# Mixture-of-experts layer on one core: rows added to the output by accumulating DMAs, in place of a last stage of gathers

## What is computed

```python
def _L0_ffn_ref(x, gamma, beta, Wr, br, W1, b1, W2, b2):
    ...
    logits = jnp.einsum('bsd,de->bse', xn, Wr) + br
    top_vals, top_idx = jax.lax.top_k(logits, K)          # K = 2
    w = jax.nn.softmax(top_vals, axis=-1)
    w_full = jnp.einsum('bsk,bske->bse', w, jax.nn.one_hot(top_idx, E, dtype=w.dtype))
    y = jnp.zeros(x.shape[:-1] + (DOUT,), x.dtype)
    for e in range(E):                                     # E = 8
        h = jax.nn.gelu(jnp.einsum('bsd,dh->bsh', xn, W1[e]) + b1[e], approximate=False)
        y_e = jnp.einsum('bsh,hd->bsd', h, W2[e]) + b2[e]
        y = y + y_e * w_full[..., e, None]
    return y
...
x = x + _L0_ffn_ref(_layernorm(x, axis=-1)[None], ...)[0]
```

## Time and profile before

| | us |
|---|---|
| median of 3 runs | 5577.97 (5570.27 to 5583.16) |
| the profiled execution | 5578.17 |
| its span, first to last instruction | 5576.4 |
| scatter of the rows (L1738 to L1742), first to last start | 4108.2 to 4427.3 |
| expert loop, first transpose to last bias add | 4468.7 to 5236.0 |
| last stage (`finish`), first POOL copy to the end of the span | 5238.2 to 5576.4 |

### The profile page before, as it was taken

How to read it: one execution, slowest core, us unless ns; L and a number is a source line. 1 busy time by engine, 2 the same in 40 slices (tenths; PEclk the granted TensorE clock), 3 DMA queues, 4 the chain that set the end, 5 groups by cost and what they waited for, 6 DMA issues and landing times. The chain is left out here.

```text
span 5576.4 us, 84757 instructions
## 1 busy us (share of the span) xinstructions
PE 3167.4 (57%) x17248; PEld 2502.8 (45%) x17249; DVE 2738.4 (49%) x6553; ACT 1159.1 (21%) x3323; POOL 2454.4 (44%) x2678
## 2 busy tenths in 40 slices
PE   4998066666666666777755551014410099999500
PEld 3775044444444555555544441003300089999500
DVE  6555344444555555666667777862220034444322
ACT  2443011111111222222211112322200023333100
POOL 3000277777777777777722223430036400000266
PEclk9999577787888888889966665555555599999755
DMA  4111644444444444444423332221123422222243
GB/s 135 57 57 59 224 125 121 121 121 121 122 123 121 121 123 123 126 125 126 125 86 91 95 91 83 81 63 38 38 72 120 143 80 71 71 70 71 85 116 112
DMA packets 427990, 564.92 MB, mean 101 GB/s; under 512 B 78180, under 2 KB 362676, under 8 KB 427806
## 3 DMA queue, kind: packets, MB, share of 16 engines
q0 software_dynamic: 94528, 263.96, 16.9%
q1 hardware_dynamic: 292398, 261.14, 16.2%
q10 hardware_dynamic: 41040, 39.59, 2.1%
HBM read 420.77 MB, written 144.88 MB: 101 GB/s over the span
## 5 line engine op out<-in xcount | busy, mean ns | idle before, releaser
L993 POOL DMA_INDIRECT rows<-node_rows,index x1564 | 1668.8, 1067 | 529.7 <-issue 468.8
L1131 PE MATMUL ps_sum<-msg,hot 128*128 128x260 f32 x3904 | 1226.7, 468 | 17.8 <-DVE big L1074 0.3
L1131 PEld LDWEIGHTS ps_sum<-msg,hot 128*128 128x128 f32 x3904 | 859.0, 232 | 179.8 <-issue 27.9
L1110 PE MATMUL ps_hot<-ident_h,hotT 128*128 128x128 bf16 x1952 | 224.7, 247 | 763.4 <-DVE hotT L1041 700.8
L1041 DVE TENSOR_SCALAR hotT<-targets,pair_node_id 128x512 bf16 x488 | 185.5, 380 | 940.5 <-SPq L956 939.1
L1065 DVE TENSOR_TENSOR msg<-rows,msg 128x1024 f32<-128x1024 f32 x488 | 601.8, 1233 | 75.4 <-ACT msg L1093 57.8
L1110 PEld LDWEIGHTS ps_hot<-ident_h,hotT 128*128 128x128 bf16 x1952 | 148.3, 110 | 942.2 <-DVE hotT L1041 684.2
L1088 ACT ACTIVATE e<-e 128x16 f32<-128x16 f32 x488 | 105.2, 216 | 1575.5 <-DVE e L1059 1570.2
L1881 DVE COPY x_rowsT<-x_ps_t 128x256 f32<-128x256 f32 x204 | 86.6, 425 | 652.1 <-PE x_ps_t L1835 652.1
L1845 PEld LDWEIGHTS x_ps_hT<-x_rowsT,x_w_now 128*128 128x128 f32 x3264 | 398.4, 193 | 12.1 <-DVE x_w_now L1892 1.7
L1845 PE MATMUL x_ps_hT<-x_rowsT,x_w_now 128*128 128x128 f32 x3264 | 399.5, 276 | 1.3 <-DVE x_w_now L1892 1.3
(11 more groups left out here) (256 smaller groups left out, 5010.4 us busy)
## 6 DMA issues: line engine op xcount, KB each, us to landing
targets<-dst_row SPq DMA_DIRECT2D x391, 128.0 KB
expert_in<-c_zeros ACTq DMA_DIRECT2D x51, 512.0 KB, 8.1
x_rows<-expert_in SPq DMA_DIRECT2D x204, 128.0 KB, 2.1
expert_out<-x_outs SPq DMA_DIRECT2D x204, 128.0 KB, 1.7
rows<-node_rows,index POOLq DMA_INDIRECT x1564
node_rows<-h_out SPq DMA_DIRECT2D x98, 132.0 KB
h_row<-node_rows SPq DMA_DIRECT2D x98, 132.0 KB, 2.1
queries<-q_out SPq DMA_DIRECT2D x98, 128.0 KB
```

What stands on the lines that cost most here:

```text
L993: g.indirect_dma_start(rows[:, j, k, :], None, s.node_rows, bass.IndirectOffsetOnAxis(ap=index[:, b, j * G + k:j * G + k + 1], axis=0)).th ...
L1110: mm = pe.transpose(ps_hot[:, j % 2, k * P:(k + 1) * P], hotT[:, j % 2, k * P:(k + 1) * P], ident_h[:, :])
L1131: mm = pe.matmul(ps_sum[:, j % 2, 0:SUM], hot[:, j % MSGS, k * P:(k + 1) * P], msg[:, j % MSGS, k, :], start=(k == 0), stop=(k == G - 1))
```

## The change

The output is now formed by additions in DRAM.

- `join` stores each finished tile of `s.sums` to the output, 98 stores on SP's queue.
- Each row in `expert_in` is four numbers longer (1,040 bytes): the number of its node, its first choice of expert, and its two weights. `route` makes this tag for all nodes, and POOL copies it behind each row before the scatter. Blank rows carry a node number past the end (12,500 plus the row's place in the tile), and the output has 128 spare rows for them.
- In the expert loop VectorE picks the weight that belongs to the tile's expert (`gates`, `choose`, `weigh`), scales the bias with it (`weigh_bias`), and `add_bias` becomes product plus weight times sum in one operation. POOL adds the 128 finished rows to the output with one indirect DMA that accumulates (`add_rows`).
- Two tiles of one expert never hold the same node, tiles of different experts may. So before an add POOL waits until all adds of the experts before are done: `adds_before` is that number per tile, and SP counts the landed adds (`track`) into `adds_done`. For the tiles after the last expert's each waits for the one before.
- `expert_out`, its stores, and the whole stage `finish` are gone. The buffers `b2_b`, `bias` and `outs` now lie in `s.big`, which is free by then.

```diff
+BLANK_TILES = 4
+XW = D + 4
...
-    s.expert_in = nc.dram_tensor("expert_in", [EX_TILES * P, D], F32).ap()
-    s.expert_out = nc.dram_tensor("expert_out", [EX_TILES * P, D], F32).ap()
+    s.expert_in = nc.dram_tensor("expert_in", [EX_TILES * P, XW], F32).ap()
...
+                g.iota(blank[:, :, D:D + 1].bitcast(I32).rearrange("p t o -> p (t o)"), [[0, BLANK_TILES]], base=N,
+                       channel_multiplier=1).then_inc(blank_set, 1)
...
+                def store(t, rows):
+                    sp.dma_start(out[bass.ds(t * P, rows), :], s.sums[0:rows, bass.ds(t, 1), 0:D].rearrange("p t d -> p (t d)")).then_inc(stored, 16)
+
+                load(0, 0, P)
+                load(1, 1, P)
+                with sp.Fori(2, TILES - 3, 2) as t0:
+                    for u in range(2):
+                        load(t0 + u, u, P)
+                        store(t0 + (u - 2), P)
                 load(TILES - 2, 0, P)
+                store(TILES - 4, P)
                 load(TILES - 1, 1, TAIL)
+                store(TILES - 3, P)
+                for t in (TILES - 2, TILES - 1):
+                    sp.wait_ge(tile_done, t + 3)
+                    store(t, P if t < TILES - 1 else TAIL)
+                sp.wait_ge(stored, 16 * TILES)
...
+                done(v.tensor_copy(s.tag[:, :, 2], gap[:, :]))
+                done(v.tensor_tensor(s.tag[:, :, 3], odds[:, :], gap[:, :], ALU.mult))
+                done(v.tensor_scalar(s.tag[:, :, 1], lowest[:, 0, :], float(EXPERTS), None, ALU.add))
...
+                    done(v.scalar_tensor_tensor(owner[:, 1 - e % 2, :], tile_id[:, :], tile_end[:, e:e + 1], owner[:, e % 2, :], ALU.is_ge, ALU.add))
+                done(v.tensor_scalar(s.expert_f[:, :], owner[:, EXPERTS % 2, :], float(EXPERTS - 1), None, ALU.min))
+                done(v.tensor_copy(s.expert_of[0:1, :], s.expert_f[0:1, :]))
+
+                for e in range(EXPERTS):
+                    done(v.tensor_scalar(owner[0:1, 0, :], tile_id[0:1, :], tile_end[0:1, e:e + 1], tiles_f[0:1, e:e + 1], ALU.is_ge, ALU.mult))
+                    done(v.tensor_tensor(first_tile[:, 1 - e % 2, :], first_tile[:, e % 2, :], owner[0:1, 0, :], ALU.add))
+                done(v.tensor_scalar(owner[0:1, 0, :], tile_id[0:1, :], tile_end[0:1, EXPERTS - 1:EXPERTS], 0.0, ALU.subtract, ALU.max))
+                done(v.tensor_tensor(first_tile[:, EXPERTS % 2, :], first_tile[:, EXPERTS % 2, :], owner[0:1, 0, :], ALU.add))
+                done(v.tensor_scalar(s.adds_before[0:1, :], first_tile[:, EXPERTS % 2, :], float(EX_TILES), None, ALU.min))
...
-                    g.wait_ge(indexed, t + 1)
+                    g.tensor_copy(rows[:, j, D:XW], s.tag[:, bass.ds(t, 1), :].rearrange("p t k -> p (t k)")).then_inc(indexed, 1)
+                    g.wait_ge(indexed, t * 2 + 2)
...
+                sp.sem_inc(adds_done, 1)
 
                 def load(n, j, turn):
 
                     row = fixed(sp, n * P)
                     from_item(sp, rowsT_psum, n, EX_RING, n - EX_RING + 1)
+                    from_item(sp, tags_read, n, EX_RING, n * 2 - 2 * EX_RING + 2)
                     sp.dma_start(rows[:, j, :], s.expert_in[bass.ds(row, P), :]).then_inc(loaded[j], 16)
 
-                def store(n, j, turn):
-                    row = fixed(sp, n * P)
-                    sp.wait_ge(out_ready, n + 1)
-                    sp.dma_start(s.expert_out[bass.ds(row, P), :], outs[:, j, :]).then_inc(stored[j], 16)
-
-                in_tiles(sp, [load, store], [0, EX_HEAD])
+                def track(n, j, turn):
+                    sp.wait_ge(added[j], turn * 16 + 16)
+                    sp.sem_inc(adds_done, 1)
+
+                in_tiles(sp, [load, track], [0, TRACK])
+
+            WEIGHTS = 16 * (EXPERTS * (2 + HC) + 1)
+
+            @block.gpsimd
+            def _(g):
+                def add_rows(n, j, turn):
+                    before = g.value_load(s.adds_before[0:1, bass.ds(n, 1)], min_val=1, max_val=EX_TILES)
+                    g.wait_ge(out_ready, n + 1)
+                    g.wait_ge(adds_done, before)
+                    g.sem_inc(s.wait_seen, 1)
+                    g.indirect_dma_start(out, bass.IndirectOffsetOnAxis(ap=token[:, j:j + 1], axis=0),
+                                         outs[:, j, :], None, compute_op=ALU.add).then_inc(added[j], 16)
+
+                in_tiles(g, [add_rows], [0])
                 for j in range(EX_RING):
-                    sp.wait_ge(stored[j], 16 * (EX_TILES // EX_RING))
-
-            WEIGHTS = 16 * (EXPERTS * (2 + HC) + 1)
+                    g.wait_ge(added[j], 16 * (EX_TILES // EX_RING))
...
-                def add_bias(n, j, turn):
-                    e = expert(v, n)
-                    v.wait_ge(out_psum, n + 1)
-                    from_item(v, stored[j], n, EX_RING, turn * 16)
-                    v.tensor_tensor(outs[:, j, :], ps_out[:, j % 2, 0:D], flat(b2_b, e, slice(0, D)), ALU.add).then_inc(out_ready, 1)
...
-                in_tiles(v, [copy_rowsT, place_w1, add_bias], [0, 0, 3])
-
-
-def finish(nc, s, out):
...
+                def gates(n, j, turn):
+
+                    v.wait_ge(loaded[j], turn * 16 + 16)
+                    v.tensor_tensor(gap[:, j:j + 1], rows[:, j, D + 2:D + 3], rows[:, j, D + 3:D + 4], ALU.subtract).then_inc(halfway, 1)
+                    v.tensor_copy(second[:, j:j + 1], rows[:, j, D + 3:D + 4]).then_inc(tags_read, 1)
+
+                def choose(n, j, turn):
+                    v.wait_ge(halfway, n * 2 + 1)
+                    v.tensor_scalar(part[:, j:j + 1], rows[:, j, D + 1:D + 2], s.expert_f[:, bass.ds(n, 1)], gap[:, j:j + 1],
+                                    ALU.is_equal, ALU.mult).then_inc(halfway, 1)
+
+                def weigh(n, j, turn):
+                    v.wait_ge(halfway, n * 2 + 2)
+                    v.wait_ge(tags_read, n * 2 + 1)
+                    v.tensor_tensor(weight[:, j:j + 1], part[:, j:j + 1], second[:, j:j + 1], ALU.add).then_inc(weighted, 1)
+                    from_item(v, added[j], n, EX_RING, turn * 16)
+                    v.tensor_copy(token[:, j:j + 1], rows[:, j, D:D + 1].bitcast(I32)).then_inc(tags_read, 1)
+
+                def weigh_bias(n, j, turn):
+                    e = expert(v, n)
+                    v.wait_ge(weighted, n + 1)
+                    v.tensor_scalar(bias[:, j, :], flat(b2_b, e, slice(0, D)), weight[:, j:j + 1], None, ALU.mult).then_inc(bias_ready, 1)
+
+                def add_bias(n, j, turn):
+                    v.wait_ge(bias_ready, n + 1)
+                    v.wait_ge(out_psum, n + 1)
+                    from_item(v, added[j], n, EX_RING, turn * 16)
+                    v.scalar_tensor_tensor(outs[:, j, :], ps_out[:, j % 2, 0:D], weight[:, j:j + 1], bias[:, j, :],
+                                           ALU.mult, ALU.add).then_inc(out_ready, 1)
+
+                in_tiles(v, [gates, copy_rowsT, choose, place_w1, weigh, add_bias, weigh_bias], [0, 0, 0, 0, 0, 3, 2])
```

More of the change, by code:

```diff
@@ L881, in _, with attend_edges @@
                                            ALU.mult, ALU.max).then_inc(step, 1)
-def attend_edges(nc, s, plan):
+def attend_edges(nc, s, plan, out):
     with ExitStack() as ctx:
@@ L1093, in weights @@
                     act.activation(msg[:, j % MSGS, :, D:SUM], e4[:, j % 2, :, :], ACT.Exp, scale=-1.0).then_inc(w_ready, 1)
[L1095 to L1098 removed]
+                act.wait_ge(blank_set, 2)
+                for a in range(0, EX_TILES, BLANK_TILES):
+                    b = min(a + BLANK_TILES, EX_TILES)
+                    act.dma_start(s.expert_in[a * P:b * P, :].rearrange("(t p) d -> p t d", p=P), blank[:, 0:b - a, :]).then_inc(blank_stored, 16)
+                act.dma_start(out[N:N + P, :], blank[:, 0, 0:D]).then_inc(blank_stored, 16)
                 in_pairs(act, [bound, copy_hot, weights], [1, 0, 1])
[L1100 removed]
+                act.wait_ge(blank_stored, 16 * (-(-EX_TILES // BLANK_TILES) + 1))
             @block.tensor
@@ L1328, in _, with join @@
                         v.sem_inc(tile_done, 1)
-def join(nc, s, x, gamma, beta, w_norm2):
+def join(nc, s, x, gamma, beta, w_norm2, out):
     with ExitStack() as ctx:
@@ L1510, in route @@
         earlier = sb("earlier", [P, P])
-        tile_id = sb("tile_id", [1, EX_TILES])
-        owner = sb("f_owner", [1, 2, EX_TILES])
+        tile_id = sb("tile_id", [P, EX_TILES])
+        owner = sb("f_owner", [P, 2, EX_TILES])
+        first_tile = sb("f_first_tile", [1, 2, EX_TILES])
         ps_t = psum("f_ps_t")
@@ L1728, in load @@
                         from_item(sp, scattered[j][k], t, 4, times)
-                    sp.dma_start(rows[:, j, :], s.ffn_in[bass.ds(row, P), :]).then_inc(loaded[j], 16)
+                    sp.dma_start(rows[:, j, 0:D], s.ffn_in[bass.ds(row, P), :]).then_inc(loaded[j], 16)
                 in_step(sp, [load], [0], TILES, 6, 4)
@@ L1753, in _, with run_experts @@
                         g.wait_ge(scattered[j][k], 16 * len(range(j, TILES, 4)))
```

(26 more changed lines are left out.)

97 lines of the change are left out of this document (19 added, 78 removed).

## The result

The changed kernel takes 5703.12 us (median of 4 runs, 5680.33 to 5709.61) against 5580.57 for the kernel before (4 runs, 5570.27 to 5590.66): ratio 1.021, 95% interval 1.018 to 1.025. It is slower. The profiled execution took 5697.41 us.

The account below looks back on a forecast made before the run. No single bound: TensorE full in the expert loop, POOL working alone in the scatter stage. 5578.2 - 333 (removed stage) + 240 (loop) + 24 (scatter) + 8 (routing) + 3 (`join`) + 8 (blank tiles) = 5528 us; range 5435 to 5715.

Parts of the forecast that it names:

- the ring works as four buffers: Rival, expert loop: adds get four tiles to land, the loop stays at 3.72 us a tile, 5288 us; chance 0.05.
- L: Expert loop: time to landing of the accumulating DMA, taken as 3.2 us, between 2.4 and 5.4; sign turns at 3.42.
- second chain: Expert loop: landing through SP's wait, next load, TensorE, VectorE to POOL's add; 6.5 + L per two tiles.
- first chain: Expert loop: landing through VectorE's token copy and sum to POOL's next add; 1.73 + L, 4.93 us a tile.
- The clock: Rival, expert loop: gaps lower TensorE's granted clock to 0.90, 5.26 us a tile, +73, 5601 us; chance 0.10.
- Routing: Routing stage: 22 more small operations, each waiting for the one before, +8 us.
- Scatter: Scatter stage: one more POOL copy per tile at 0.25 us, 98 times, +24 us; +98 with a second full wait.
- `join`: 98 stores on SP's queue, each after a tile's loads, fitting in the gap; +3 us in all.
- The borders between experts: Expert loop: at seven borders an add waits for all earlier adds, already landed by then; 0 us.
- +8 for blank tiles: End of expert loop: the last four tiles each wait for the add before, about +8 us after the last matmul.
- The removed stage: Last stage: 340.4 us from the loop's last bias add to the end go, less landing and closing; net -333 us.
- The blank rows: Edge stage: longer blank rows, iota and extra ScalarE DMA lie under POOL's gathers; 0 us.

Follow-up runs that it names:

- experiment 4: Changed kernel with accumulation left out, each add a plain scatter that overwrites the row: 5531.14 us, ratio 0.9925 to the kernel before, 4.955 us a tile.
- after: The changed kernel itself, with no further edit: 5703.12 us, ratio 1.021 to the kernel before.
- experiment 5: Changed kernel with TensorE's read of the expert's number moved ahead of the transposes: ratio 1.0075 to the kernel before, 5.363 us a tile, on a slower chip.
- 6: Changed kernel with SP counting landed adds eight tiles late and TensorE's expert-number read ahead of the transposes: 5624.66 us, ratio 1.0083 to the kernel before.
- experiment 1: Changed kernel with SP counting landed adds eight tiles late in place of four: 5624.31 us, ratio 1.0085 to the kernel before, 5.352 us a tile.
- experiment 7: Changed kernel with four extra unread TensorE transposes per tile: ratio 1.0131 to the kernel before, 5.466 us a tile, on a slower chip.
- experiment 10: experiment 3 with the blank ids made in the first stage and copied where the iota stood: 5280.69 us, ratio 0.947 to the kernel before.
- experiment 9: experiment 3 with blank rows stored as 488 stores of 64 rows inside ScalarE's pair loop: 5688.44 us, ratio 0.9549 to the kernel before, on a slower chip.
- experiment 3: Changed kernel with eight expert-loop buffers and SP counting adds eight tiles late: 5285.85 us, ratio 0.948 to the kernel before, 3.718 us a tile.

## Why the prediction was wrong

**The mechanism was right.** One add in flight behind the token copy, and the same landing ahead of the next load through SP: the period rose, TensorE fell to 78% busy, and cutting each chain alone and both together gave what two such chains give. The rival "the ring works as four buffers" is out: it needed eight buffers and a late track.

**The steps that failed are two terms of its sum, each too small: the landing L, and the fixed part of the second chain.** Each alone turned the sign. With L = 3.8 in place of 3.2 and nothing else changed the prediction's own sum is 5655 us. With 7.45 + L for two tiles in place of 6.5 + L, and L left at 3.2, the tile is 5.33 us, the loop +326, and the sum 5528 - 240 + 326 = 5614 us. Both are slower than before. In the loop as measured, which goes by the second chain, the 0.6 us of L are worth 0.3 us a tile, 61 us, and the 0.95 us of the fixed part 0.475, 96 us: about 157 of the 161 us by which the loop was underpriced. (This split is worked out from the terms; experiment 4 supports the first part, 0.74 us a tile for 1.4 us of landing.)

**L.** The prediction took 3.2 us for the landing; measured 3.8, with a spread of only 3.6 to 4.1. The estimate counted only the bytes of the second read (0.2 us) and what a load takes over a store (0.4); it left POOL's own part as it was, and that grew by 0.6, from 0.96 to 1.56 us. That the landing is later by just this time is argued, not shown. Experiment 4 gives the sign back by taking the accumulation out alone. By the fit in the Trainium skill ("DMA: Bandwidth & Descriptors", Anatomy of one DMA) it would be an estimated 2.3 us. With the second read of the Trainium skill's "Collectives: The Full Stack" (The bandwidth ceiling) added to the scatter's 2.6 the prediction had estimated 3.0. The plain scatter's 2.4 in experiment 4 agrees with the first; for the accumulating one the measured 3.8 stands against both.

**The second chain was priced too low.** It was put at 6.5 + L for two tiles, so below the first. The rows of after make it 11.25, so 7.45 + L. Most of the missing part is on TensorE: the working went through VectorE's copies (2.6 us from the transposes to the sum), but the longer branch is transposes, 0.69 us of reading the expert's number, and `down`, 3.3 us. That read was there before, hidden while TensorE had queued matmuls; with the queue empty it showed. Experiments 5 and 6 show that taking it out of this chain brings the tile down to the first chain's 5.35 us, and that outside the chain it costs nothing. The load went out 0.67 us after the landing in that row, not 0.44.

**The first chain was priced too high**, 1.73 + L where experiment 1 makes it 1.45 + L: VectorE started the token copy 0.03 us after the landing, not 0.23 (5005.48 and 5005.51 in that run), and the sum starts 0.10 us after the token copy's start. So the prediction's 5.53 us a tile and 5655 us for L = 3.8 come near the measured 5.70 and 5703 partly by luck: the chain that they were worked out from stood at 5.35, and the other one set the time.

**The clock** was a rival of 0.10 and came true in a small way, 0.93 granted in the loop, worth 0.23 us a tile by experiment 7. The prediction had named a clock under 0.97 as its sign. It doesn't add up with the two chains: 5.35 and 5.55 alone, 5.70 together, 5.47 together at full clock. So part of the 0.35 us that experiment 1 won came with the clock, which rose to 1.00 there. How the two chains and the clock share the last 0.15 us is not settled.

**The other terms.** Routing +8.5 for +8. Scatter +15.2 for +24: the second copy does not wait for the first one's end and adds 0.13 to 0.15 us, not 0.25:

```profile
4202.59 0.20 POOL L1768 COPY g_index<-slot 128x2 int32 x1
4202.72 0.19 POOL L1769 COPY g_rows<-tag 128x4 f32 x1
4203.72 0.99 POOL L1773 DMA_INDIRECT expert_in<-g_rows,g_index  x1 [0.82 <-POOL g_rows L1769]
...
4205.98 0.20 POOL L1768 COPY g_index<-slot 128x2 int32 x1
```

4205.98 - 4202.59 = 3.39 us, against 3.24. `join`: about 2 for 3 (its last addition of the input started 314.6 us after the first, instead of 312.4). The borders between experts cost nothing, as said: POOL waited for the count (SPq L1863) only 3 times, 8.8 us, and these are the last three adds, at 5676.65, 5681.16 and 5685.60, the "+8 for blank tiles". The removed stage gave 324.6 net of that, for 333 - 8.

**The blank rows were priced at 0**, on the ground that POOL's gathers set the edge stage. At its start ScalarE does: +11.1 us to the first sum. At the stage's end little of this is left. Away from the slower chip the last sum started at 2838.9, 2823.0, 2835.7, 2833.8, 2834.6, 2821.1, 2820.5, 2819.2 and 2837.8 us in nine profiled runs with the blank rows, and at 2819.1 in the profile of before. That is 0 to 20 us, and it doesn't follow the edits. So of the 17.6 us before the routing, about 2 are `join`, and how much of the rest is the change's stays open.

## What to carry to other kernels

A ring hides a landing only for the steps that lie, in the engine's program order, between the release and the first instruction that waits for it; count these steps on every in-order queue the landing passes (here VectorE's and SP's), not the buffers, and a ring made deeper on one of them alone gained next to nothing here (5.70 to 5.55, where both brought 3.72). When work moves into a loop as a DMA, ask first whether its landing can be kept off every chain: then an uncertain latency doesn't matter (3.8 or 2.4 us, 3.72 us a tile either way), and if it can't, the forecast hangs on a number that no row shows and should be priced at its slow end. When a full engine starts to have gaps, its own register reads and waits, hidden until then, join the path.

## What the runs showed of the hardware

- An accumulating indirect DMA of 128 rows of 1 KB in float32 takes POOL 1.56 us and lands after 3.8; the same DMA without the accumulation 0.97 and 2.4.
- Between the end of a POOL memset and an iota behind it 6.94 us passed ("issue"); a copy in the iota's place started 0.07 us after the memset (experiment 10), and the first sum of the stage came 4.5 us earlier.
- 51 stores of 520 KB hold ScalarE's queue for 84 us; as 488 small ones among the gathers they freed 46 us at the start of the edge stage, and its end came 27 to 44 us later (experiment 9).
- One chip moved less in the edge stage than another (104 GB/s in 1000 to 3100 us of experiment 5, against 122 in 1000 to 2800 of after), with the full expert loop of experiment 3 at 3.718 us a tile on both.
